# Causal attention: where the diagonal score blocks get their mask

## The reference, cut to what matters

```
h = _layernorm(x, ln_w, ln_b)            # then a causal convolution of 3 taps per channel
qkv = h @ attn_w ; q, k, v = split       # then rotary embedding of q and k
scores = jnp.einsum('bqhd,bkhd->bhqk', q, k) / jnp.sqrt(jnp.float32(D))
causal = jnp.tril(jnp.ones((T, T), dtype=bool))
scores = jnp.where(causal, scores, jnp.float32(-1e+30))
p = jax.nn.softmax(scores, axis=-1)
y = jnp.einsum('bhqk,bkhd->bqhd', p, v).reshape(B, T, C)
return y @ proj_w
```

## Time and profile before

| | |
|---|---|
| median of 3 runs | 2719.34 us (2717.33 to 2720.9) |
| the profiled execution | 2720.97 us, its span 2719.2 us |
| busy, PE / PEld | 2300.0 us (85%) / 1182.8 us (43%) |
| busy, DVE / ACT / POOL | 1966.7 (72%) / 1825.6 (67%) / 1315.7 (48%) |
| mean granted TensorE clock | 0.952 of 2.4 GHz |
| causal attention after its maxima, batch 0 | 1808.0 to 1909.7 us |
| the same, batch 1 | 2049.2 to 2151.4 us |
| one exp over 128 x 1024 (L1741) | median 1014 ns |
| one mask product (L1703) | median 219 ns, 256 in all |

### The profile page before, as it was taken

One profiled execution on the slowest core, in us unless ns is written; L12 is line 12 of the kernel. 1 busy time (PEld: TensorE's weight loads), 2 busy tenths in 40 slices (PEclk: granted clock), 3 DMA queues, 4 the chain that ended last, 5 costly groups with the idle time before them and its releaser, 6 DMA issues. The chain is left out here.

```text
span 2719.2 us, 38745 instructions
## 1 busy us (share of the span) xinstructions
PE 2300.0 (85%) x12428; PEld 1182.8 (43%) x12429; DVE 1966.7 (72%) x1849; ACT 1825.6 (67%) x2850; POOL 1315.7 (48%) x517
## 2 busy tenths in 40 slices
PE   7788888888898888888888986779878989998988
PEld 2344444444434444444443522322422355555547
DVE  7899999999978999999997557752592222224554
ACT  5999999999969999999996353127305621112256
POOL 2199998999915999989996110000000040000010
PEclk8999999999998999999999888789978989999999
DMA  2510001000025000110000030001001150011000
GB/s 100 140 31 27 27 27 40 27 27 27 20 89 122 28 27 27 27 40 27 27 27 26 2 94 32 2 9 43 13 1 36 47 229 20 23 67 35 4 6 31
DMA packets 58297, 112.66 MB, mean 41 GB/s; under 512 B 13251, under 2 KB 19267, under 8 KB 57168
## 3 DMA queue, kind: packets, MB, share of 16 engines
q1 hardware_dynamic: 49408, 98.24, 11.6%
q0 software_dynamic: 8784, 13.03, 1.6%
HBM read 84.97 MB, written 25.97 MB: 41 GB/s over the span
## 5 line engine op out<-in xcount | busy, mean ns | idle before, releaser
L1487 POOL TENSOR_TENSOR hs<-hs,c_bc 128x2048 f32<-128x2048 f32 x256 | 1166.4, 4556 | 66.0 <-DVE hs L1538 50.5
L1538 DVE TENSOR_TENSOR_SCAN hs<-decays,ps 128x512 f32<-128x512 f32 x512 | 611.0, 1216 | 28.1 <-PE ps L1565 10.5
L1538 DVE TENSOR_TENSOR_SCAN hs<-decays,carry,ps 128x512 f32<-128x512 f32 x512 | 621.6, 1270 | 10.6 <-PE ps L1565 9.6
L1573 PE MATMUL ps<-hs,sel 128*64 128x512 f32 x2048 | 500.9, 610 | 14.5 <-POOL hs L1487 14.2
L1565 PE MATMUL ps<-ident,dbu_even 128*128 128x128 f32 x2048 | 297.2, 284 | 95.2 <-DVE hs L1538 63.1
L1565 PE MATMUL ps<-ident,dbu_odd 128*128 128x128 f32 x2048 | 294.8, 283 | 92.2 <-DVE hs L1538 61.5
L1501 ACT ACTIVATE decays<-delta_far,A 128x512 f32<-128x512 f32 x512 | 360.5, 718 | 12.2 <-DVE hs L1538 12.1
L1501 ACT ACTIVATE decays<-delta_near,A 128x512 f32<-128x512 f32 x512 | 358.3, 711 | 2.4 <-DVE hs L1538 2.4
L1509 ACT ACTIVATE dbu_odd<-du_turned,b_turned 128x512 f32<-128x512 f32 x512 | 359.3, 714 | 0.0
L1509 ACT ACTIVATE dbu_even<-du_turned,b_turned 128x512 f32<-128x512 f32 x496 | 348.0, 714 | 0.0
L1565 PEld LDWEIGHTS ps<-ident,dbu_even 128*128 128x128 f32 x2048 | 221.9, 143 | 245.2 <-DVE hs L1538 192.0
(11 more groups left out here) (323 smaller groups left out, 2643.2 us busy)
## 6 DMA issues: line engine op xcount, KB each, us to landing
c_bc<-c_rows SPq DMA_DIRECT2D x256, 128.0 KB, 2.8
o_rows<-osb SPq DMA_DIRECT2D x26, 256.0 KB
u_rows<-u SPq DMA_DIRECT2D x4, 1024.0 KB, 4.4
d_rows<-delta SPq DMA_DIRECT2D x4, 1024.0 KB, 4.2
delta_near<-d_rows SPq DMA_DIRECT2D x4, 1024.0 KB, 10.1
hs<-u_rows SPq DMA_DIRECT2D x4, 1024.0 KB, 6.8
delta_far<-d_rows SPq DMA_DIRECT2D x4, 1024.0 KB, 13.0
w_down<-in_expert_proj SPq DMA_DIRECT2D x1, 4096.0 KB, 39.4
```

The costliest lines, as they stand in the source:

```text
L1487: pool.tensor_tensor(x, x, spread(c_bc[:, g, :], 4), ALU.mult).then_inc(weighed.sem, 1)
L1538: dve.tensor_tensor_scan(hs[:, quad % RING, n, :], decays[:, s % RING, :], ps[:, DBU + s % RING, :], carry[:, at(i * GB, g), blk] if q els ...
L1573: mm = pe.matmul(ps[lo:lo + DB, ACC + quad % 2 * 2 + j // 2, :], k.sel2[:, :], hs[:, quad % RING, j, :], start=False, stop=False, skip_gro ...
```

## The change

The mask products of the diagonal steps are gone; the score products count `score` themselves. VectorE makes a matrix `limit` once for each batch: -1e30 where the key comes after the query, +1e30 elsewhere (2 x `early_query` + 1e30). For each half of a diagonal step it waits for the two score products, and takes the minimum of the two banks' 128 x 128 blocks and `limit`, in place in PSUM. It counts `causal_only`, for which ScalarE's exp of that half now waits in place of `score`. VectorE's order is written out: ahead of the wait for the sums of group n stand the minima of the steps from the group's second one to the first step of group n+1, since TensorE computes the scores of that step before the last sums of group n.

```diff
+    on_diagonal = [s for s, (job, qc, group, t, *_) in enumerate(steps_of) if causal and t * P >= qc * W]
+    limited = {m: n for n, m in enumerate(2 * s + half for s in on_diagonal for half in range(2))}
+    causal_only, limit_made = k.sig("causal_only"), k.sig("limit_made")
+    limit = k.sb("limit", [P, P], ctx=ctx) if causal else None
...
-                diag = causal and t * P >= qc * W
...
-                    mm = pe.matmul(ps[0:krows, 2 * (m % 3) + j % 2, first:W], job.kx[rows, par, c, t * P:t * P + krows],
-                                   job.qx[rows, par, c, qc * W + first:(qc + 1) * W], start=True, stop=True)
-                    if not diag:
-                        mm.then_inc(score.sem, 1)
-                for j in range(4 if diag else 0):
-                    m = 2 * s + j // 2
-                    mm = pe.matmul(ps[:, 2 * (m % 3) + j % 2, first:first + P], k.ident16[:], k.early_query[:],
-                                   start=False, stop=True, skip_group_check=True)
-                    mm.then_inc(score.sem, 1)
+                    pe.matmul(ps[0:krows, 2 * (m % 3) + j % 2, first:W], job.kx[rows, par, c, t * P:t * P + krows],
+                              job.qx[rows, par, c, qc * W + first:(qc + 1) * W], start=True, stop=True)\
+                      .then_inc(score.sem, 1)
...
-                act.wait_ge(score.sem, score.at(2 * m + 2))
+                if m in limited:
+                    act.wait_ge(causal_only.sem, causal_only.at(limited[m] + 1))
+                else:
+                    act.wait_ge(score.sem, score.at(2 * m + 2))
...
+            def limit_early(s):
+                first = steps_of[s][4]
+                for m in (2 * s, 2 * s + 1):
+                    if m in limited:
+                        x = ps[:, 2 * (m % 3):2 * (m % 3) + 2, first:first + P]
+                        dve.wait_ge(score.sem, score.at(2 * m + 2))
+                        dve.tensor_tensor(x, x, spread(limit[:], 2), ALU.min).then_inc(causal_only.sem, 1)
+
+            if causal:
+                dve.tensor_scalar(limit[:], k.early_query[:], 2.0, -NEG, ALU.mult, ALU.add)\
+                   .then_inc(limit_made.sem, 1)
+                dve.wait_ge(limit_made.sem, limit_made.at(1))
             for n in range(NG):
+                for s in range(ends[n - 1] + 1 if n else 0, min(ends[n] + 1, NS)):
+                    limit_early(s)
                 dve.wait_ge(used.sem, used.at(ends[n]))
```

More of the change, by code:

```diff
@@ L1792, in attention @@
     score.passed(4 * NS)
+    causal_only.passed(len(limited))
+    limit_made.passed(1 if causal else 0)
     weighed.passed(2 * NS)
```

## The result

The changed kernel took 2734.45 us in the median of six runs (2729.14 to 2741.46), the kernel before 2719.95 in six runs beside it (2717.33 to 2721.47). The ratio is 1.0055, interval 1.0038 to 1.0071: slower by 15 us. The profiled execution took 2736.07 us (span 2734.3).

A forecast was written before the change was run, and what follows sets the result against it. Diagonal steps were taken as bound by latency along scores, exp and next scores, not by VectorE's room. 16 groups at +0.63 us gave +10.1, less 1.5, plus 0.3: +8.9 us, median 2728.2 us, range 2721 to 2744.

The forecast's parts named there:

- The duration of the minimum, 0.42 us: VectorE's minimum in diagonal steps, 256 elements per partition in PSUM: taken as 0.42 us from the 256-element row.
- a = 0.45 us: Addition to each diagonal step's path from scores to first exp by minimum and signal: 0.45 us, bounds 0.32 and 0.72.
- The 0.19 us that the change takes away: In each diagonal step, the four mask products were said to delay the exp by 0.19 us.
- The four steps: Warm group of four diagonal tiles: 2.73, 2.30, 1.88, 1.46 us, together 8.37 against 7.74, so +0.63 us a group.
- TensorE's freed time buys nothing more: Diagonal steps: TensorE's freed 0.33 us gains nothing beyond the 0.14 us of each step already counted.
- rivals 2 and 3: Smaller addition to diagonal steps: no difference (a = 0.36, 2722.4 us, chance 0.17); faster (a = 0.20, 2712.2 us, chance 0.06).
- The first, cold group: Each batch's first diagonal group, at 1.2 GHz: near -0.1 instead of +0.6 us, -1.5 us for both batches.
- Taps ahead of a minimum, once, +0.3: Batch 0, VectorE's queue: copy and two long convolution taps delay the next group's second-tile minimum once, +0.3 us.
- The reciprocal: VectorE's 3.35 us reciprocal and its product, ahead of later minima in attention: hidden with 2.9 us to spare.
- The sum: Whole kernel: 10.1 - 1.5 + 0.3 = +8.9 us, median 2728.2 us, 0.33% slower.
- Rival 1, the clock: TensorE's clock falls in diagonal stretches: +18 us, 2746 us, in half the warm groups; 2765 in all; chance 0.13.
- Rival 4: Minima wait in VectorE's queue behind copies, taps and normalisation: at worst +13 us on top, 2741 us; chance 0.09.

The follow-up runs named there:

- e2_no_mask: Changed kernel without minima or mask products, exponential at scale 0 in diagonal steps, causality not computed; 2696.08 us, 0.9943 of the kernel before.
- e3_split: Changed kernel, but TensorE masks the first half of each diagonal step by two products, VectorE's minimum the second; 2708.85 us, 0.9985 of the kernel before.
- the two repeats: The changed kernel run again twice without edit; 2727.11 us, ratio 1.0054, and 2725.11 us, ratio 1.0037 to the kernel before.
- the two lengthened kernels: Kernel before plus twelve and seven useless TensorE products ending batch 0's and 1's attention phases, run twice; 2723.22 us (1.0032) and 2721.05 us (1.0029).
- e1_repeat: The changed kernel run again without edit; 2727.11 us, 1.0054 of the kernel before.
- e4_twice: Changed kernel with the first half's minimum done twice in a row in each diagonal step; 2761.6 us, 1.0171 of the kernel before.

## Why the prediction was right, and where it was off

**The duration of the minimum, 0.42 us.** Measured 0.427 (128 operations). The row of the 256-element copy gave it, although that one does not write to PSUM. The Trainium skill, "VectorE: DVE Perf Modes", section on the TRN2 errata, by its table estimates 0.39, too little; by its line of 151 cycles plus the elements 0.42, and the measurement sides with that one.

**The addition a = 0.45 us.** Measured 0.47 in the first step: exp 1.67 after the scores, 1.20 without masks (e2_no_mask). The signal from VectorE to ScalarE took 0.04 us, not 0.03. Doubling the minimum added 0.46 to 0.47 again, so nothing hides it; and a minimum off the path, on the second half alone (e3_split), delays nothing. That the minimum on the path is the cause is thereby shown from both sides: taken out, doubled and moved off the path, it changes the step as it should.

**The 0.19 us that the change takes away.** The size is right (e2_no_mask), its reading was not: I put it down to four mask products, and it is the price of the two of the first half (e3_split). The sum does not change by it.

**The four steps.** Predicted 2.73, 2.30, 1.88, 1.46, together 8.37; measured 2.75, 2.31, 1.90, 1.46, together 8.42. With query half 1 it is the same: by the starts of the exponentials, four unmasked and four masked tiles took 16.85 us and take 17.53. So +0.68 in each of the 14 warm groups where I had +0.63, by the start of one group to the start of the next: 0.7 us in all.

**TensorE's freed time buys nothing more.** Right: in the changed kernel every row of scores waits for an exponential, and the 0.33 us a step which TensorE saves appears only as idle time before the scores. Without minima TensorE ends last again in the second step, so that the group is 6.67 and not the 6.57 by which rivals 2 and 3 were priced.

**The first, cold group: about -0.1.** Not to be told by these runs. Measured, from the first scores to those of the next group, against the kernel before: +0.70 and -0.42 in the first profile, +0.01 and +0.11, +0.14 and +0.20 in the two repeats, a mean of +0.12. But the kernel before varies as much with nothing changed: 10.37 and 10.88 us in its profile, 10.22 and 10.88, 10.87 and 10.39 in the two lengthened kernels, whose first groups are the same. A mean near -0.1 is thus no confirmation. My argument for the second step held: it went from 3.76 us to 3.46, and to 3.29 in e1_repeat, and TensorE's own products ended it. What I had left out is that TensorE reaches its full clock at a place that varies: the third step's scores took 1.24 us in the first profile of the changed kernel, 0.71 in its repeat and in the kernel before. That less work moves that place is not shown.

**Taps ahead of a minimum, once, +0.3.** Right in place, 0.2 in size: two long taps end where the minimum starts.

```profile
1837.95 1.52 DVE L2129 SCALAR_TENSOR_TENSOR hc<-HN,ffn_vec,hc 128x511 f32<-128x511 f32 x2
1839.39 0.76 DVE L1765 TENSOR_TENSOR ps<-ps,limit 128x256 f32<-128x256 f32 x2
```

The reciprocal was hidden as worked out: it and its product had ended 2.85 us before the next minimum began.

**The sum.** +8.9 predicted; the phases grew by 10.4, 10.3 and 10.5 us in three profiles. Of the 1.5 us between, 0.7 is the 0.05 a group, and 0.4 the cold groups (2 x 0.22, as uncertain as they are); the taps take 0.1 off. The last 0.4 is a step that the sum treated like the others. In the fourth step of a group I set off the 0.14 us by which TensorE's own work had delayed the next scores; but behind the last step of a phase no scores follow, and its later and longer pair of exponentials counts in full. From the first scores of the last group to the end of its last exponential it was 16.93 us and is 17.81 in both batches: +0.88, which is 0.20 more than +0.68, twice. The median moved by 14.5 us in the first comparison, 13.0 and 10.4 in the other two; the last, with most runs, is the one that agrees with the phases. So the forecast for the phases was 1.5 us low, and the first median lay another 4 us above what the phases explain. In the profiled execution such an excess, 4.7 us, stood in untouched stages; that the medians have theirs from there too is likely, and not shown. These stages vary from one execution to the next in all profiles: the first scan 643.7 to 648.0 us, cross attention 48.5 to 53.4, the row maxima 93.0 to 101.3.

**Rival 1, the clock.** It did not come true in the changed kernel, but its mechanism exists: with one more minimum per step the clock fell (e4_twice, in its one profile). I had given it 0.13; the changed kernel is one 0.43 us operation a step away from it. The warning of the Trainium skill, "TensorE: Matmul & The Clock Gate", section on psum-queue depth-cycling, holds for e4_twice and not for the changed kernel.

**Rivals 2 and 3** needed a under 0.36; it was 0.47. **Rival 4**, VectorE's queue as the bound: only the one late minimum above.

## What to carry to other kernels

Moving a short operation from a busy engine to an idle one is priced by the path, not by the busy share: here VectorE had three quarters of its time free, and the exchange replaced 0.19 us on the way to the exp by 0.47. Ask which half of the data is needed first: the same minimum on the half that is needed one exponential later is free, and an additive mask can be written before the scores instead of after them, which took the 0.19 us off the way to the exp and cost 0.09 ahead of the scores. And a control that fills time with products also feeds the clock of the stage behind it.

## What was not expected of the hardware

- Two mask products behind the scores delayed their reader by 0.19 us. Put first, they did not delay it (exp 1.20 after the scores), but the scores themselves started 0.09 later.
- TensorE's clock stayed at 1.00 for 93 us with the engine busy for 73% and 84% of two stretches, and fell to 0.50 in the kernel with 0.47 us more of waiting per step, in some groups and not in others of the same shape.
- Once, in ten profiles, ScalarE started to read TensorE's result 12 us after the products had ended, and 0.45 us after the last of GpSimd's indirect DMA instructions. Its cause is open.
- The sort stage took either 20.7 or 22.4 us, nothing between, in ten profiles of seven kernels, with TensorE's busy time 16.2 or 17.8 us in it.
